# A top-2 mixture-of-experts kernel on one core: a rewritten prologue, three tiles with an fp32 down product, and a reordered last turn

## The chip, the core and the metric

The kernel runs on one core of one Trainium2 chip. The core's engines work side by side, each on its own queue of instructions in program order: TensorE (PE; its weight loads are PEld) multiplies into PSUM, VectorE (DVE), ScalarE (ACT) and GpSimd (POOL) do elementwise work, and DMAs are issued from the queues of SyncE (SP), ScalarE and GpSimd. Engines wait for each other by semaphores. The metric is the device time of one execution in microseconds (us); lower is better.

## What is computed

```python
# x (2,1024,256); weight (256,256); router_w (8,256); lang_w (4,256)
# w1 (8,256,1024), b1 (8,1024); w2 (8,1024,256), b2 (8,256)
ys = cond * 256**-0.5
d = rsqrt(einsum('bi,io->bo', ys*ys, weight*weight) + 1e-8)
y = einsum('bsi,io->bso', x * ys[:, None, :], weight) * d[:, None, :]
lang = softmax(y @ lang_w.T + lang_b);  lp = pad(lang, one zero)
idx = arange(8) % 4
logits = y @ router_w.T + router_b + 0.1 * (lp[..., idx] + lp[..., idx + 1])
top_p, top_i = top_k(softmax(logits), 2);  top_p = top_p / top_p.sum(-1)
h = gelu(einsum('bsd,edh->bseh', y, w1) + b1)        # exact gelu
expert_out = einsum('bseh,ehd->bsed', h, w2) + b2
out = x + sum over the two chosen experts of top_p * expert_out
```

## The kernel before

2048 tokens stand in 16 tiles of 128. Each goes to two of eight experts; the 4096 places are sorted by expert into 39 tiles of 128 (`NT`), some partly filled. Tile j of the first eight belongs to expert j, so that the code knows its expert; the other tiles look theirs up in the table `te`.

**Precision.** The large products are made of float16 pairs. Each weight matrix is a "half" n (n = 2e is w1 of expert e, n = 2e + 1 its w2), comes from HBM in fp32 (1 MB) into a staging place `PLACE[n]` and is split into a high part (`split_high`, ScalarE, L641) and a low part (`split_low`, VectorE, L779). Each needs a power-of-two scale, from a bound on the half: TensorE multiplies 16 column blocks with themselves (`gram`, L460), ScalarE sums (`gram_sums`), TensorE adds over partitions (`sum_squares`), VectorE makes the scale (`scale_weights`). The order of the low splits is `LOW_ORDER`. The hidden h of a tile is split likewise in two halves g of four chunks: GELU (L684), high part (`high_h`), low part (`low_h`, L945), both times a scale out of `cur`. A down product takes three float16 products of 256 columns a chunk (high by high, high by low, low by high); from tile 8 on two instructions cover them.

**Prologue.** SyncE loads cond, the adaLN weight, the router rows, x in four pieces of 512 KB, then halves 0 to 3; later ones wait for a place. Place 4 to 9 are laid over the buffers of x and of the prologue. TensorE transposes x in pairs of tiles (`transpose_x`, L411) and the router rows; VectorE forms the demodulation d, the combined weight Wyr (L747, L752), and TensorE computes the rows of y with their 12 logits (`rows_of_y`, L445), fp32. ScalarE squares x for the scale of y (`square_x`). y is split and written to `y_rows` in HBM. Then VectorE alone walks the routing: language softmax, two picks, counts per expert (through TensorE), the base of every expert's tiles, each token's slot (L869 to L878), two one-hot arrays (`tilehot`, `onehot`), which TensorE multiplies into the list `idx` of token numbers by slot (L510). The gates are computed between these steps on VectorE and written to `y_rows`. GpSimd gathers the rows of tile j by an indirect DMA (L350), five ahead.

**Main loop.** Turn j on TensorE: transpose tile j + 2 (L525, one PSUM bank, so it waits for the copy `copy_x` of the tile ahead), block up (j+1, 0) with down (j-1, 1), block up (j+1, 1) with down (j, 0); in turns 1 to 3 the Gram of one expert in the middle. Up (j, g) with j < 8 waits for split 2j of `LOW_ORDER`, down for split 2j + 1 and for the low part of h. VectorE's and ScalarE's turns are written out by hand at the end of their blocks. `rows_out` (L955, L960) scales the down result and adds b2; GpSimd multiplies by the gate (L368) and adds the rows to `out` by an indirect DMA (L373), one at a time. `expert_table(j)` copies the scales into `cur` and waits, from tile 3 on, until GpSimd's gate multiply of tile j - 3 is done (`o_ready`). The first scatter waits for the copy of x to `out` (`x_copied`).

## Time and profile before

| | |
|---|---|
| median of three runs | 326.2 us (326.15 to 326.49) |
| the profiled execution | 324.92 us, its span 323.1 us |
| PE busy | 280.9 us (87%) |
| ACT / DVE / POOL busy | 210.5 / 197.2 / 173.8 us |
| share of the chain that ended last | PE 65%, DMA 8%, DVE 7%, POOL 6%, issue 5%, ACT 5% |
| moved by DMA | 35.72 MB |

### The profile page before, as it was taken

What the parts mean: (1) busy time and instruction counts of PE and PEld (TensorE: products, weight loads), DVE (VectorE), ACT (ScalarE), POOL (GpSimd) and SP (SyncE); (2) the same over time, 40 slices, a digit from 0 to 9 for tenths busy, and PEclk for the clock granted to TensorE, in tenths of its full rate; (3) what the DMA queues carried; (4) which work ended last, traced back from release to release, by engine and by line L of the source; (5) the groups of instructions that cost most, each with busy time, mean ns of one, the idle gap of its engine ahead of it and who ended that gap; (6) DMA issues with size and microseconds to landing.
All of it is one profiled execution on the core that took longest, in us unless ns stands there. A gap on an engine that the chain in (4) does not pass through costs nothing.

```text
span 323.1 us, 9091 instructions
## 1 busy us (share of the span) xinstructions
PE 280.9 (87%) x3118; PEld 233.7 (72%) x3118; DVE 197.2 (61%) x461; ACT 210.5 (65%) x457; POOL 173.8 (54%) x140
## 2 busy tenths in 40 slices
PE   6889957859969966999999999999999999999900
PEld 4867856559859964888888888888888878888600
DVE  1227787479775895665756666665756666675610
ACT  2657489895669967767675757667675757667400
POOL 3040000640782896686677676768677675746460
PEclk9599985897989999999999999999999999999985
DMA  4987998189932112233323223242323223231220
GB/s 145 374 301 233 366 370 247 50 311 361 358 96 35 19 35 50 36 48 55 58 46 52 52 39 64 35 68 36 58 46 50 53 40 63 37 51 18 32 21 11
DMA packets 25480, 35.72 MB, mean 111 GB/s; under 512 B 4112, under 2 KB 21984, under 8 KB 25280
## 3 DMA queue, kind: packets, MB, share of 16 engines
q1 hardware_dynamic: 17584, 24.73, 22.2%
q0 software_dynamic: 7488, 10.39, 19.9%
q8 instruction: 29, 0.48, 0.6%
q10 hardware_dynamic: 368, 0.04, 0.1%
q14 instruction: 11, 0.09, 0.1%
HBM read 27.61 MB, written 9.64 MB: 115 GB/s over the span
## 4 chain that ended last, share of the span: by engine, by line
PE 65%; DMA 8%; DVE 7%; POOL 6%; issue 5%; ACT 5%; SPq 1%; ACTq 0%; DVEq 0%; POOLq 0%
PE ps L533 28%; PE ps L547 26%; POOL onehot L368 5%; PE ps L445 4%; DMA wsp<-in_L_ffn_w 4%; DVE wsp L779 3%; ACT wsp L641 3%; PE ps L525 2%; DMA out<-onehot,idx 2%; DMA wsp<-in_x 2%; PE ps L411 2%; ACT pay L684 1%; DVE pay L945 1%; POOL out L373 1%; PE ps L515 1%
## 5 line engine op out<-in xcount | busy, mean ns | idle before, releaser
L533 PE MATMUL ps<-onehot,wsp 128*128 128x128 f16 x1872 | 159.3, 221 | 7.0 <-DVE wsp L779 6.2
L533 PEld LDWEIGHTS ps<-onehot,wsp 128*128 (+1 forms) x1872 | 133.1, 97 | 37.9 <-DVE wsp L779 7.5
L684 ACT ACTIVATE pay<-ps,cur 128x128 f32<-128x128 f32 x312 | 117.4, 457 | 62.4 <-issue 43.6
L547 PE MATMUL ps<-wsp,pay 128*128 (+1 forms) x688 | 152.0, 313 | 0.1
L368 POOL TENSOR_SCALAR onehot<-onehot,cur 128x256 f32<-128x256 f32 x39 | 50.1, 1285 | 63.7 <-DVE onehot L960 34.4
L945 DVE SCALAR_TENSOR_TENSOR pay<-pay,cur 128x512 f16<-128x512 f32 x78 | 59.1, 757 | 40.6 <-ACT pay L673 38.5
L373 POOL DMA_INDIRECT out<-onehot,idx x39 | 71.2, 1827 | 14.1 <-POOL onehot L368 8.1
L350 POOL DMA_INDIRECT rows<-y_rows,idx x39 | 46.0, 1179 | 48.5 <-DVE idx L899 36.9
L547 PEld LDWEIGHTS ps<-wsp,pay 128*128 128x128 f16 x688 | 55.3, 97 | 3.1 <-issue 0.5
L673 ACT ACTIVATE pay<-pay,cur 128x512 f16<-128x512 f32 x47 | 34.0, 723 | 1.5
L939 DVE TENSOR_SCALAR pay<-pay,cur 128x512 f16<-128x512 f32 x31 | 17.5, 565 | 27.5 <-ACT pay L684 27.5
L955 DVE SCALAR_TENSOR_TENSOR onehot<-ps,cur,b2bc 128x256 f32<-128x256 f32 x39 | 18.8, 483 | 3.9 <-PE ps L547 2.4
L641 ACT ACTIVATE wsp<-stage,wscale 128x2048 f16<-128x2048 f32 x8 | 15.7, 1997 | 5.2 <-DVE wsp L779 4.0
L779 DVE SCALAR_TENSOR_TENSOR wsp<-wsp,wscale 128x2048 f16<-128x2048 f32 x8 | 18.8, 2347 | 0.0
L779 DVE SCALAR_TENSOR_TENSOR wsp<-stage,wscale,wsp 128x2048 f16<-128x2048 f32 x8 | 18.8, 2345 | 0.0
L525 PE MATMUL ps<-ident,rows 128*128 128x128 f32 x78 | 15.0, 274 | 3.1 <-DVE onehot L922 2.5
L460 PE MATMUL ps<-wsp 128*128 128x128 bf16 x128 | 11.5, 263 | 7.0 <-DMA wsp<-in_L_ffn_w 6.2
L445 PE MATMUL ps<-wsp,pay 128*128 128x268 f32 x64 | 16.3, 397 | 1.4 <-DVE wsp L803 0.7
L641 ACT ACTIVATE wsp<-wsp,wscale 128x2048 f16<-128x2048 f32 x8 | 15.7, 2000 | 1.1 <-DVE wscale L772 1.0
L460 PEld LDWEIGHTS ps<-wsp 128*128 128x128 bf16 x128 | 10.4, 120 | 7.6 <-DMA wsp<-in_L_ffn_w 4.5
L960 DVE SCALAR_TENSOR_TENSOR onehot<-ps,cur,onehot 128x256 f32<-128x256 f32 x31 | 15.0, 484 | 1.1
L525 PEld LDWEIGHTS ps<-ident,rows 128*128 128x128 f32 x78 | 9.7, 144 | 7.1 <-issue 3.5
(164 smaller groups left out, 181.9 us busy)
## 6 DMA issues: line engine op xcount, KB each, us to landing
stage<-in_L_ffn_w SPq DMA_DIRECT2D x8, 1024.0 KB, 11.5
wsp<-in_L_ffn_w SPq DMA_DIRECT2D x8, 1024.0 KB, 10.4
wsp<-in_x SPq DMA_DIRECT2D x4, 512.0 KB, 8.1
y_rows<-pay SPq DMA_DIRECT2D x4, 512.0 KB, 10.3
b2bc<-in_L_ffn_b SPq DMA_DIRECT2D x1, 1024.0 KB, 10.2
rows<-y_rows,idx POOLq DMA_INDIRECT x39, 2.9
out<-onehot,idx POOLq DMA_INDIRECT x39
wsp<-in_L_cond_weight SPq DMA_DIRECT2D x1, 256.0 KB, 2.9
```

The source lines that it names most:

```text
L350: g.indirect_dma_start(out=rows[:, j % ROWS, :], out_offset=None, in_=y_rows, in_offset=bass.IndirectOffsetOnAxis(ap=idx[:, j:j + 1], axis ...
L368: g.tensor_scalar(outb[:, j % RING, :], outb[:, j % RING, :], cur[:, j % RING, C_P:NCUR], None, ALU.mult).then_inc(o_ready, 1)
L373: g.indirect_dma_start(out=out, out_offset=bass.IndirectOffsetOnAxis(ap=idx[:, j:j + 1], axis=0), in_=outb[:, j % RING, :], in_offset=None ...
L445: last = mm(ps[:, t % BANKS_Y, 0:WIDTH_Y], xT[:, t, k * P:(k + 1) * P], Wyr[:, t // TB, k, :], start=(k == 0), stop=(k == KD - 1))
L525: last = tr(ps[:, XB, k * P:(k + 1) * P], rows[:, j % ROWS, k * P:(k + 1) * P], ident[:, :])
L533: last = mm(ps[:, HB + (2 * j + g) % RING, c * P:(c + 1) * P], wsp[:, bass.ds(e, 1), o:o + P].rearrange("p a f -> p (a f)"), xsp[:, j % RI ...
L547: last = mm(ps[:, OB + j % 2, 0:width], hsp[:, (2 * j + g) % NH, part, c, :], wsp[:, bass.ds(e, 1), o + w:o + w + width].rearrange("p a f ...
L641: a.activation(parts_of(n)[0], staged(n), ACT.Copy, scale=wscale[:, n:n + 1]).then_inc(w_high, 1)
L673: a.activation(hsp[:, (2 * j + g) % NH, 0, :, :].rearrange("p c n -> p (c n)"), h32[:, g, :], ACT.Copy, scale=cur[:, j % RING, C_H:C_H + 1 ...
L684: last = a.activation(h32[:, g, c * P:(c + 1) * P], ps[:, HB + (2 * j + g) % RING, c * P:(c + 1) * P], ACT.Gelu, bias=cur[:, j % RING, cc: ...
L779: v.scalar_tensor_tensor(out=lo, in0=staged(n), scalar=wscale[:, n:n + 1], in1=hi, op0=ALU.mult, op1=ALU.subtract).then_inc(w_split, 1)
L945: v.scalar_tensor_tensor(out=lo, in0=h32[:, g, :], scalar=cur[:, j % RING, C_H:C_H + 1], in1=hi, op0=ALU.mult, op1=ALU.subtract).then_inc( ...
```

## The change

- **x** comes in five pieces (2, 2, 4, 4, 4 tiles). A tile now holds the tokens p * 8 + t of a batch instead of t * 128 + p, so that a partition's tiles are adjacent in HBM. cond and the router rows are issued on ScalarE's queue, b1 and the biases on SyncE's behind x.
- **Start**: the router rows are transposed ahead of x, R is copied behind dcol. The scale of y comes from the largest |x| (`max_of_x`, five VectorE reductions) instead of ScalarE's squares. Tile pair 4 of x is transposed among the rows of y. GpSimd's large iota waits for nothing.
- **Loads**: halves 0, 2, 4, 6, 1, 7 at once; 3 after the first piece of y is written; 8, 9, 5 after the last; b2's broadcast, which stood behind half 5, after three gathers; then 10 to 13, the copy of x to `out`, 14 and 15. Half 14 waits for split_low(10), half 15 for split_low(11).
- **Grams** in groups of two or three halves (`GROUPS`); two groups ahead of the routing, two after the mapping, three in the loop (turns 1, 2, 4). From the third group on VectorE takes the largest entry (`gram_max`) instead of ScalarE's sum. Warm products 6 instead of 12.
- **Routing**: bases by five steps over an 8 x 8 mask instead of logarithmic sums; TensorE also adds the home tile; onehot last, in four pieces; gates on GpSimd and ScalarE, written to `y_rows` from ScalarE's queue.
- **Tiles 0 to 2** (`DIRECT`): the down product is one fp32 product of 256 columns per chunk, of the unsplit GELU result and the staged w2. No high_h, no low_h, no wait for splits 1, 3, 5; those follow later, in `SPLIT_ORDER`.
- high_h(j, 1) is on VectorE for all tiles from 3 on (before from 8 on).
- **Last turn**: rows_out(37) is VectorE's first step of turn 38, and the gates of tiles 37 and 38 are multiplied on ScalarE (`weigh`).

The core of the diff:

```diff
-WARM = 12
-PLACE = (0, 1, 2, 3, 4, 5, 6, 7, 8, 9, 0, 2, 4, 5, 1, 3)
-LOW_ORDER = (0, 2, 1, 4, 3, 6, 5, 8, 7, 10, 9, 12, 11, 14, 13, 15)
+WARM = 6
+DIRECT = 3
+PLACE = (0, 7, 1, 4, 2, 5, 3, 6, 8, 9, 0, 1, 2, 3, 0, 1)
+SPLIT_ORDER = (0, 2, 4, 6, 7, 8, 1, 9, 10, 11, 12, 13, 3, 5, 14, 15)
+SPLITS = {0: (6, 7), 1: (8, 1), 2: (9, 10), 3: (11, 12), 4: (13, 3), 5: (5, 14), 6: (15,)}
+HIGHS = {0: (8, 1), 1: (9, 10), 2: (11, 12), 3: (13, 3), 4: (5,), 5: (14, 15)}
+GROUPS = ((0, 2, 4), (6, 7), (8, 9), (1, 3, 5), (10, 11), (12, 13), (14, 15))
+GRAMS = {1: 4, 2: 5, 4: 6}
...
 # SyncE, behind the loads of 8, 9 and 5
             for j in range(RING):
                 sp.wait_ge(gathered[j], 16)
+            sp.dma_start(b2bc[:, :, :].rearrange("p e d -> p (e d)"), ...)
+            for n in (10, 11, 12, 13):
+                load_weights(n)
             for b in range(NB):
                 sp.dma_start(out[b * SEQ:(b + 1) * SEQ, :], x[b]).then_inc(x_copied, 16)
-            for n in (10, 11, 14, 12, 15, 13):
+            for n in (14, 15):
                 load_weights(n)
...
 # TensorE, down_step and its waits
+                if j < DIRECT:
+                    return mm(ps[:, OB + j % 2, 0:D], hraw[:, (2 * j + g) % NH, c, :], staged(2 * j + 1)[:, cc, :],
+                              start=(cc == 0), stop=(cc == KF - 1))
...
+                    if j < DIRECT:
+                        pe.wait_ge(w_in[PLACE[2 * j + 1]], 16)
+                        pe.wait_ge(gelu_done, 2 * j + g + 1)
...
 # ScalarE, split_high
+                if n in (12, 13):
+                    wait_split(act, 8)
+                    wait_split(act, 9)
+                if n in (14, 15):
+                    wait_split(act, 3)
+                    wait_split(act, 5)
+                    act.wait_ge(l2_done, 3)
...
 # GpSimd, the gates
+            pool.wait_ge(best, 1)
+            g.tensor_tensor(pex, lg[:, :, 0:E], over(s1[:, 3, :], E), ALU.subtract).then_inc(p_in, 1)
+            pool.wait_ge(second, 1)
+            g.tensor_tensor(pe1[:, 0, :], s1[:, 4, :], s1[:, 3, :], ALU.subtract).then_inc(p_in, 1)
+            pool.wait_ge(p_exp, 2)
+            g.tensor_scalar(pe1[:, 2, :], pe1[:, 1, :], 1.0, None, ALU.add).then_inc(p_sum, 1)
...
 # VectorE, the counts to the bases
+            step(v.tensor_scalar(tl[:, 0, :], ps[:, 3, 0:E], -(P / 2 + 0.5), 1.0 / P, ALU.add, ALU.mult))
+            step(v.tensor_scalar(tl[:, 1, :], tl[:, 0, :], MAGIC, MAGIC, ALU.add, ALU.max))
+            step(v.scalar_tensor_tensor(out=tmask[:, :, :], in0=tl[:, 1:2, :].broadcast_to([P, E, E]), scalar=-MAGIC,
+                                        in1=before[:, :, :], op0=ALU.add, op1=ALU.mult))
+            step(v.tensor_reduce(base[:, 0, :], tmask[:, :, :], AX.X, ALU.add))
+            step(v.tensor_tensor(base[:, 1, :], base[:, 0, :], over_base[:, :], ALU.add))
...
 # VectorE, the turns
             for j in range(NT):
-                if j >= EARLY:
+                if j == NT - 1:
+                    rows_out(j - 1)
+                if j >= DIRECT:
                     high_h(j)
-                low_h(j, 1)
+                    low_h(j, 1)
```

Where things stand in a row, at three places.

VectorE at the start, before: the copy of R (it waits for the router rows' transposition, which is behind x on TensorE) is ahead of the root chain.

```order
L729 TENSOR_SCALAR dv<-ps 128x4
L731 COPY R<-ps 128x24
L733 RECIPROCAL dv<-dv 128x4
L734 TENSOR_TENSOR dv<-dv 128x4
L735 TENSOR_TENSOR dv<-dv 128x4
L736 TENSOR_SCALAR dv<-dv 128x4
L738 TENSOR_TENSOR dcol<-dv 128x4
L742 TENSOR_TENSOR Rd<-R,dcol 128x2x12 x2
L747 SCALAR_TENSOR_TENSOR wsp<-wsp,ys,ps 128x256 x4
```

And after:

```order
L784 TENSOR_SCALAR dv<-ps 128x4
L786 RECIPROCAL dv<-dv 128x4
L787 TENSOR_TENSOR dv<-dv 128x4
L788 TENSOR_TENSOR dv<-dv 128x4
L789 TENSOR_SCALAR dv<-dv 128x4
L791 TENSOR_TENSOR dcol<-dv 128x4
L794 COPY R<-ps 128x24
L797 TENSOR_TENSOR Rd<-R,dcol 128x2x12 x2
L802 TENSOR_REDUCE xmax<-wsp 128x1 x2
L810 SCALAR_TENSOR_TENSOR wsp<-wsp,ys,ps 128x256 x4
```

R moved behind dcol, and two reductions of x came ahead of Wyr.

VectorE at the end of the routing, before (wsp is `tilehot` in L884 and L887), where TensorE's mapping products wait for L887:

```order
L876 TENSOR_REDUCE slot<-wsp 128x32
L877 TENSOR_SCALAR slot<-slot 128x32
L878 TENSOR_SCALAR slot<-slot 128x32
L884 TENSOR_TENSOR wsp<-wsp,slot 128x1248
L885 TENSOR_TENSOR onehot<-wsp,slot 128x4096
L887 TENSOR_TENSOR wsp<-wsp,tok 128x1248
```

And after:

```order
L939 TENSOR_REDUCE slot<-wsp 128x32
L940 TENSOR_SCALAR slot<-slot 128x32
L941 TENSOR_SCALAR slot<-slot 128x32
L947 TENSOR_TENSOR wsp<-wsp,slot 128x1248
L949 TENSOR_TENSOR wsp<-wsp,tok 128x1248
L953 TENSOR_TENSOR onehot<-wsp,slot 128x128x8 x4
```

onehot moved to the end and became four pieces.

ScalarE from the GELUs (5, 0) of turn 4 on, before (L684 GELUs, L673 high_h, L669 copy_x, L631 gram_sums, L641 split_high, here of halves 14 and 15):

```order
L684 ACTIVATE pay<-ps,cur 128x128 x4
L673 ACTIVATE pay<-pay,cur 128x512
L641 ACTIVATE wsp<-stage,wscale 128x2048
L684 ACTIVATE pay<-ps,cur 128x128 x4
L673 ACTIVATE pay<-pay,cur 128x512
L669 ACTIVATE onehot<-ps 128x256
L684 ACTIVATE pay<-ps,cur 128x128 x4
L673 ACTIVATE pay<-pay,cur 128x512
L641 ACTIVATE wsp<-stage,wscale 128x8x256
```

And after, from the same GELUs on (L736 GELUs, L724 high_h, L720 copy_x, L695 split_high of 14 and 15):

```order
L736 ACTIVATE pay<-ps,cur 128x128 x4
L724 ACTIVATE pay<-pay,cur 128x512
L736 ACTIVATE pay<-ps,cur 128x128 x4
L720 ACTIVATE onehot<-ps 128x256
L695 ACTIVATE wsp<-stage,wscale 128x2048
L736 ACTIVATE pay<-ps,cur 128x128 x4
L724 ACTIVATE pay<-pay,cur 128x512
L695 ACTIVATE wsp<-stage,wscale 128x8x256
```

The high split of half 14 moved from turn 4 to turn 5, ahead of the GELUs (6, 0), and high_h of (5, 1) left this queue.

## Rows read from the trace of the kernel before

**Rows 1.** TensorE's waits: what waited for whom, total us, times, longest.

```profile
PE ps L533 <- DVE wsp L779: 6.2, 4, 3.3
```

**Rows 2.** Timeline of the start: start us, us, engine, line, operation, [idle before].

```profile
2.42 2.25 SPq L285 DMA_DIRECT2D wsp<-in_x  x4
...
6.45 0.21 ACT L601 ACTIVATE dv<-dv 128x4 f32<-128x4 f32 x1 [0.60 <-DVE dv L729]
...
9.16 1.94 PE L411 MATMUL ps<-ident,wsp 128*128 128x128 f32 x8 [2.95 <-DMA wsp<-in_x]
...
15.06 1.65 DVE L747 SCALAR_TENSOR_TENSOR wsp<-wsp,ys,ps 128x256 f32<-128x256 f32 x4 [2.11 <-PE ps L428]
...
17.15 2.04 PE L445 MATMUL ps<-wsp,pay 128*128 128x268 f32 x8 [0.68 <-DVE wsp L752]
...
22.72 0.55 ACT L646 ACTIVATE pay<-ps,yscale 128x256 f16<-128x256 f32 x1 [3.25 <-DVE yscale L762]
...
37.00 0.22 DVE L813 TENSOR_REDUCE s<-wsp 128x16 f32<-128x64 f32 x1
```

**Rows 3.** Timeline from the routing chain to the first gathered rows.

```profile
40.88 0.16 DVE L770 TENSOR_SCALAR wround<-ps 128x2 f32<-128x2 int32 x1
...
44.79 0.16 DVE L845 TENSOR_SCALAR tli<-ps 128x8 int32<-128x8 f32 x1
...
50.40 2.29 DVE L885 TENSOR_TENSOR onehot<-wsp,slot 128x4096 f16<-128x4096 int16 x1
...
53.46 2.85 PE L510 MATMUL ps<-wsp,onehot 128*128 128x39 f16 x32 [0.23 <-DVE wsp L887]
...
56.72 0.20 DVE L899 SCALAR_TENSOR_TENSOR idx<-ps,wsp 128x39 uint32<-128x39 f32 x1
...
57.86 2.37 POOL L350 DMA_INDIRECT rows<-y_rows,idx  x1 [36.91 <-DVE idx L899]
...
60.99 2.75 PE L515 MATMUL ps<-onehot,ones 128*128 128x512 f16 x12
...
63.58 0.38 PE L525 MATMUL ps<-ident,rows 128*128 128x128 f32 x2
```

**Rows 4.** Busy time by stretch (PE, PEld, DVE, ACT, POOL), TensorE's clock, DMA share, GB/s.

```profile
58.00:60.00 2.00, 1.72 (x17) 1.45 (x14) 1.17 (x1) 2.00 (x2) 2.00 (x1) 0.59 0.00 0
```

**Rows 5.** Groups by line, 63.4 to 135 us: count, busy us, mean ns, idle before.

```profile
L684 ACT ACTIVATE pay<-ps,cur 128x128 f32<-128x128 f32 x68 | 25.5, 455 | 7.9 <-PE ps L533 4.4 <-DVE cur L932 2.1 <-issue 1.4
L779 DVE SCALAR_TENSOR_TENSOR wsp<-wsp,wscale 128x2048 f16<-128x2048 f32 x8 | 18.8, 2347 | 0.0
...
L945 DVE SCALAR_TENSOR_TENSOR pay<-pay,cur 128x512 f16<-128x512 f32 x16 | 11.9, 746 | 11.0 <-ACT pay L673 10.0 <-issue 1.1
...
L641 ACT ACTIVATE wsp<-wsp,wscale 128x2048 f16<-128x2048 f32 x4 | 8.0, 1999 | 1.1 <-DVE wscale L772 1.0
```

**Rows 6.** Timeline of turns 2 to 7, TensorE.

```profile
92.39 1.09 PE L460 MATMUL ps<-wsp 128*128 128x128 bf16 x16 [3.04 <-DMA wsp<-in_L_ffn_w]
...
97.63 0.28 PE L465 MATMUL ps<-wsum,ones 128*128 128x2 f32 x2
...
119.95 0.52 PE L533 MATMUL ps<-onehot,wsp 128*128 128x128 f16 x6 [0.78 <-DVE wsp L779]
...
120.63 0.51 PE L533 MATMUL ps<-onehot,wsp 128*128 128x128 f16 x6
...
128.66 0.41 PE L525 MATMUL ps<-ident,rows 128*128 128x128 f32 x2 [2.50 <-DVE onehot L922]
```

**Rows 7.** DMA: issues with median us to landing; spread of the weight loads' line.

```profile
out<-in_x SPq DMA_DIRECT2D x2, 8.1
...
DMA to landing us min/median/max: 4.9/11.3/14.0
```

**Rows 8.** Last turn: scatter 36 in the timeline, scatter 37 in the chain of waits.

```profile
302.97 1.83 POOL L373 DMA_INDIRECT out<-onehot,idx  x1 [0.28 <-POOL onehot L368]
...
308.01 3.69 DMA out<-onehot,idx
```

More of the change, by code:

```diff
@@ L120, in adaln_moe @@
         first = sb("first", [P, E], I32)
-        home = sb("home", [P, E], I32)
+        eids = sb("eids", [P, E], I32)
+        homes = sb("homes", [P, E], F16)
+        over_base = sb("over_base", [P, E], I32)
+        before = sb("before", [P, E, E])
         tok1 = sb("tok1", [P, K * T], I32)
@@ L574, in _ @@
             transpose_rows(0)
+            sum_squares(2)
             transpose_rows(1)
@@ L871, in _ @@
-            step(v.tensor_tensor(r2[:, :, :], rank, eq[:, :, :], ALU.add))
-            step(v.tensor_tensor(eq[:, :, :], r2[:, :, :], each(home[:, :]), ALU.add))
+            step(v.scalar_tensor_tensor(out=eq[:, :, :], in0=ps[:, RB, 0:T * E].rearrange("p (t e) -> p t e", e=E),
+                                        scalar=float(P), in1=each(base[:, 1, :]), op0=ALU.is_ge, op1=ALU.mult))
+            step(v.tensor_tensor(eq[:, :, :], ps[:, RB, T * E:2 * T * E].rearrange("p (t e) -> p t e", e=E), eq[:, :, :],
+                                 ALU.add))
```

498 lines of the change are left out of this document (269 added, 229 removed).

## The prediction

> **What bounds the kernel now.** First the table of TensorE's waits [rows 1]: in 323.1 us it waits for others only near the start and in the first eight turns; from 130 us on no wait is listed. A faster start therefore shifts everything behind it, and a change of the first turns is worth what it does to the moment at which the waits end. The timeline then gives four marks. The combined weight Wyr is ready and the rows of y begin at 17.15; VectorE's routing chain begins at 37.00; the indices are written at 56.72 to 56.92; the first gathered rows are transposed at 63.58 [rows 2, 3]. I forecast each mark. Below, u is the time since the first transposes of gathered rows. Before, turn 7 begins with its transposes at 128.66, u = 65.1 [rows 6], and turn 8 begins at u = 71.5 (transposes and a wait to 129.73, then two blocks of 2.7).
>
> **To the rows of y.** Before, TensorE sits 2.95 us and starts on x at 9.16; behind that on its queue stands the transposition of the router rows, and behind that VectorE's copy of R and the whole root chain, so the 1.65 us that build Wyr run from 15.06 only [rows 2]. After, the router rows go ahead of x and R behind dcol. The root that dcol needs is taken at 6.45 [rows 2], so it comes near 7.5. x in pieces of 256 KB is issued 1.2 us sooner than the first 512 KB before (2.42 [rows 2], and three small loads less ahead). What remains is x: TensorE must do pieces 0 and 1 before the dcol products (1.9 us at the low clock, 0.9 at the high one), and piece 2 before the router products. New on VectorE are five reductions of x, two ahead of Wyr, of 512 elements each; the products of Wyr take 0.41 for 256 [rows 2], so between 0.41 and 0.82, and I take 0.6. With x there at 6 to 7.5 us: transposes to 9, dcol products to 10, Wyr 1.65 and its router part, 12 us; 11 if nothing is late, 14.5 if the clock falls as it did before. I take 12.5, since the router rows are now third on ScalarE's queue and could land late. **Gain 4.4 (2.5 to 5.9).**
>
> **The rows of y.** Before, 17.15 to 37.00: 5.6 us to the first scaled tile (22.72) and 14.3 of tiles bound by TensorE [rows 2]. After, three reductions of x (1024 elements, by the same row 0.8 to 1.6, taken as 1.1 each) stand ahead of the scale, which TensorE's own queue mostly hides (it reaches that place 3.2 us after the start, they take 3.5), plus one small multiply; and one more transposition pair (0.45) falls among the tiles. Cost 0.8. The routing chain begins at 33.3: 12.5 + 20.8. **Gain 3.7 (1.5 to 5.5).**
>
> **The routing chain, 19.9 us before.** Step by step on VectorE [rows 3]: the first scale_weights inside the first pick goes (0.35). The second scaling, the third and the gap subtraction leave the place between the choice and the counts: the counts are taken at 44.79, 0.9 after the choice, and what stands there now (a reciprocal 0.25, one scaling 0.45) is as long as the way over TensorE, gain about 0.1. From the counts to the table of bases 2.7 us of 14 small steps become five steps of 0.16 to 0.25, 1.15: gain 1.55. One of the full-width adds goes (0.33), as TensorE adds the home tile itself; its 33 products instead of 16 take 1.5 us and end just ahead of the bases, at no cost. Then tilehot, its multiply and onehot were 3.75 us before TensorE's 32 mapping products (2.85) could start [rows 3]. Now onehot (2.29) comes last in four pieces, and eight products follow each piece: after the last piece 0.7 remains instead of 2.85, with about 0.4 for three more instructions and the wait. Gain 1.75. Sum 4.1; I take 3.6, as products (0.71 per eight at the low clock) are longer than pieces (0.6). ScalarE's part must not be late: GpSimd subtracts, ScalarE takes two exponentials, GpSimd adds, all beside the second pick, and the reciprocal has about 1 us to spare. The indices at 16.3 after the chain's start: 49.6. **Gain 7.3 in all.**
>
> A row and a rule: the first gather lasted 2.37 us instead of 0.96 beside a split_low that began before it [rows 3]. The Trainium skill, "SBUF — State Buffer", section Who interferes with whom, says that a VectorE instruction with two SBUF inputs shuts out GpSimd instructions that read SBUF, but infers that descriptor writing isn't shut out. The row speaks for the wider reading. By the rule alone the gather would save 1.4 us, hidden by the next term, and the sum stays.
>
> **From the indices to the first transposes, 6.7 before.** Two things run: the gather (0.9 until it starts, then held by split_low(0), which in the new order begins about 1.4 after the indices: data some 6.3 to 6.6 after them) and TensorE's own queue. That now holds five Gram halves (8, 9, 1, 3, 5) and six warm products. The clock was low when the mapping products began at 53.46 and rose about 6 us later [rows 3, 4]; again TensorE has little to do from the choice on, so I take it as low, and as rising about 6.2 us after the first mapping products. That makes 1.8 halves at 1.9 us and 3.2 at 0.96, and six warm products at 0.23 [rows 3]: 7.9 after the mapping, 7.3 after the indices. TensorE is last, not the gather. Cost 0.7. First transposes at 56.9. **Gain 6.6 (3 to 9).**
>
> **The first turns.** Prices [rows 5]: split_low 2.35 (VectorE), split_high 1.94 back to back (ScalarE), low_h 0.75, four GELUs 1.5; six up and three down products 0.67 [rows 6], so a block 2.7. The down product of tiles 0 to 2 in fp32: one pass of 256 columns for each of eight chunks. The row of fp32 products with 268 columns gives 0.46 each [rows 2], so 0.44 and 3.5 a tile against 2.7: TensorE gets 0.8 more three times. Hidden, since TensorE waits there anyway. It takes away the waits for splits 1, 3 and 5, and six low_h. But all 16 splits are still due by turn 7, and 11 of ScalarE's are now left at u = 0, where before it were 7: the five high splits after routing end 5 us before the rows come, and ScalarE then stands still.
>
> I followed the three queues with these prices, in u. ScalarE from 3.0: GELUs, copies and splits 8, 1, 9, 10, 11 end with high_h(3) at 25.8. VectorE: splits 2, 4, 6, 7, 8, 1 until 17.8, tables to 19.3, then expert_table(3), which needs tile 0's scatter path and so the copy of x to the output. VectorE's low_h(3,0) waits for 25.8 anyway; split_low(10) and the scales of 12 and 13 end 29.5; only then may ScalarE split 12 and go on to the GELUs of (3,1), which end 33. VectorE stood still 3 us. From 33 it is full: two parts of h, splits 11, 12, 13, 3, 5, tables: 54.2. ScalarE may not split 14 before split 5 is low (53.7), and GELUs (6,0) come behind that: h(6,0) at 57.8, low_h 58.6, **split_low(14) ends at u = 61**, 3.6 us of standing still included. Turn 6 of TensorE waits for exactly this from 52.6 on; before, the like wait ended at 119.95, u = 56.4. After it, the old order lost another 3.9 us (split 13, then VectorE's copy_x(8) with a 2.5 us wait) [rows 1, 6]; the new one has nothing left but one split and runs two turns of 5.6. Turn 8 then begins at 72.2, plus the low clock after an 8 us wait. Before, after 3.04 us of waiting, half a Gram and a block took 5.2 (92.39 to 97.63) instead of 3.7 [rows 6], 1.5 more; I take 1.8 (1.5 to 3.1). So turn 8 at u = 74.0 against 71.5: **loss 2.5**.
>
> **The steady turns** are unchanged. **The last turn**: scatters form a chain, 302.97 then 308.01, each 3.7 to landing and 0.75 to the next start [rows 8]. With rows_out(37) ahead of the last split and ScalarE's multiply in place of GpSimd's, scatter 37 can start at 302.97 + 4.45 = 307.4. The last down product comes 0.65 later through the same move, still ahead of its scatter. **Gain 0.6.** That the tiles take tokens eight apart changes addresses of gathers and scatters, not their number: nothing, or up to 0.3 us per scatter, hidden but for two.
>
> **Sum**: -6.6 + 2.5 - 0.6 = -4.7 (rounded up) against the profiled execution, 324.9 to 320.2. The median of the runs is 326.2, 1.3 above that execution; the same difference gives 321.5.
>
> **Rivals.** A, the loop fits together better than by hand. For: of the 61 us to split_low(14) VectorE works 51; the 10 us of standing still are couplings that shift with small delays. If half goes, split_low(14) ends at 56 and turn 8 begins near 68: 315.5. If all goes, TensorE's own 52.6 decides, turn 8 begins at 63.8: 311.3. B, slower than before: the copy of x to the output. Before, it was issued right after three gathers and took 8.1 us [rows 7]. Now it stands behind b2's broadcast and four weight loads, the last of which waits for split_low(6) (u = 9.4), so 7 MB are under way from u = 4. At the rate of the weight loads (about 400 GB/s) it lands at 22, which is where VectorE can still bear it (22.7). Every us beyond that delays expert_table(3) and all behind it one for one: from 27 the gain is gone, and at 250 GB/s it lands at 32: 331. C, the start doesn't get shorter: x is not there sooner, or TensorE's clock falls in the start; then nothing of the 3.7 is left at the routing chain, the rest as above: 325.2. One DMA more: the load of half 15 waits for split_low(11) (36.8) and needs 4.9 at least [rows 7]; its Gram comes at 42, TensorE waits 4 us in turn 4, and this is inside the calculation, because VectorE is later still.
>
> **Chances.** Forecast (319 to 325) 0.52; A (311 to 318) 0.25; C 0.10; B 0.13. A measurement of this kernel can tell 0.2% (0.65 us) from no change; by the same cases faster 0.79, same 0.07, slower 0.14. The range 313 to 327.5 leaves out the far end of A and half of B, and a slow loop beside a slow start.
>
> **What would show it.** The y rows should begin at 12.5 and the routing chain near 33; the indices 16.3 after that; TensorE's clock low in the mapping; the first transposes at 57, right behind the warm products, with no wait for the gather. In the turns, VectorE should be idle before high_h(3) and before low_h(6,0), and TensorE's longest wait should be for split_low(14) in turn 6. If VectorE is instead idle at expert_table(3) for long, it is B. If turn 8 begins under 70 us after the first transposes, my reading of the couplings is wrong and A holds. If the y rows begin after 15, the first term is wrong.

## The result, and the profile after

| | median, us | runs |
|---|---|---|
| before | 326.12 (323.71 to 328.05) | 20 |
| after | 323.89 (321.89 to 326.9) | 20 |

The ratio is 0.994, with a 95% interval of 0.9919 to 0.996: the change makes the kernel 1.3 to 2.6 us faster. (The ratio leaves out three of the changed kernel's 20 runs, which lay over 1.5% above its fastest.) In a later group of runs it was 0.9958 (0.9925 to 0.999). The forecast of 321.5 us had the sign right and the size more than twice too large: 4.7 us less were forecast, some 2 are there, and 1.4 by the later group.

The profiled execution of the changed kernel took 323.72 us, with a span of 321.9. TensorE's waits, with total us, times and longest us, say where it now stands still (L553 is the mapping at the end of the routing and L527 a step among the rows of y, the other three are in the turns):

```profile
PE ps L576 <- DVE wsp L852: 7.4, 1, 7.4
PE ps L553 <- DVE onehot L953: 4.4, 1, 4.4
PE ps L496 <- DMA stage<-in_L_ffn_w: 3.4, 1, 3.4
...
PE ps L568 <- DMA rows<-y_rows,idx: 1.8, 1, 1.8
PE ps L527 <- DVE bmx L859: 1.2, 1, 1.2
```

[Rows 1] showed four waits for splits (L779 there, L852 here) with 3.3 us as the longest. Now there is one of 7.4 us. The timeline shows the marks up to the first gathered rows, to be read beside [rows 2, 3]:

```profile
12.88 2.04 PE L482 MATMUL ps<-wsp,pay 128*128 128x268 f32 x8 [0.41 <-DVE wsp L815]
...
27.26 0.27 PE L527 MATMUL ps<-ident,bmx 128*8 128x128 f32 x1 [1.24 <-DVE bmx L859]
...
34.85 0.22 DVE L891 TENSOR_REDUCE s<-wsp 128x16 f32<-128x64 f32 x1
...
51.31 0.20 DVE L962 SCALAR_TENSOR_TENSOR idx<-ps,wsp 128x39 uint32<-128x39 f32 x1
...
57.09 1.46 PE L558 MATMUL ps<-onehot,ones 128*128 128x512 f16 x6
58.38 0.38 PE L568 MATMUL ps<-ident,rows 128*128 128x128 f32 x2
```

And the same timeline at turns 1 to 6, in order of time, ScalarE's, VectorE's and TensorE's rows together:

```profile
82.99 0.17 DVE L1005 COPY cur<-tab 128x11 f32<-128x11 f32 x1 [5.34 <-POOL onehot L406]
...
89.45 2.00 ACT L695 ACTIVATE wsp<-stage,wscale 128x2048 f16<-128x2048 f32 x1 [3.94 <-DVE wscale L845]
...
101.83 1.47 PE L496 MATMUL ps<-stage 128*128 128x128 bf16 x16 [3.41 <-DMA stage<-in_L_ffn_w]
...
113.38 2.00 ACT L695 ACTIVATE wsp<-stage,wscale 128x2048 f16<-128x2048 f32 x1 [4.67 <-DVE wsp L852]
...
117.56 0.75 DVE L1019 SCALAR_TENSOR_TENSOR pay<-pay,cur 128x512 f16<-128x512 f32 x1 [3.87 <-ACT pay L724]
118.23 2.34 DVE L852 SCALAR_TENSOR_TENSOR wsp<-stage,wscale,wsp 128x2048 f16<-128x2048 f32 x1
...
120.63 0.82 PE L576 MATMUL ps<-onehot,wsp 128*128 128x128 f16 x6 [7.41 <-DVE wsp L852]
...
128.66 0.38 PE L568 MATMUL ps<-ident,rows 128*128 128x128 f32 x2
...
134.27 0.38 PE L568 MATMUL ps<-ident,rows 128*128 128x128 f32 x2
```

Turn 7 begins at 128.66 us in both of these profiles [rows 6]: all that the prologue won, 5.2 us at the first transposes, has been paid back by then. Turn 8 begins at 134.27 instead of 135.2, because the old order lost time once more in turn 7 (the wait at 128.66 in [rows 6]). The last scatter starts at 311.26.

### The profile page after: what moved, and what is told of

Its sections match the earlier page's. It is cut to its first block, busy times and chain, and to the rows that moved or that the text cites. A ratio compares the mean times of both kernels' runs of the same rounds, so it can differ in the third digit from the quotient of the medians.

```text
span 321.9 us, 9020 instructions
## 1 busy us (share of the span) xinstructions
PE 281.6 (87%) x3103; PEld 234.6 (73%) x3103; DVE 201.4 (63%) x462; ACT 195.9 (61%) x419; POOL 164.9 (51%) x145
## 4 chain that ended last, share of the span: by engine, by line
PE 49%; POOL 16%; issue 10%; DVE 9%; DMA 9%; ACT 2%; SPq 1%; POOLq 0%; DVEq 0%; ACTq 0%
PE ps L576 20%; PE ps L593 18%; POOL out L413 8%; POOL onehot L406 5%; PE ps L482 4%; DMA out<-onehot,idx 4%; DMA out<-in_x 4%; POOL rows L387 3%; DVE wsp L852 3%; DMA wsp<-in_x 2%; PE ps L496 2%; PE ps L568 2%; SPq L338 1%; PE ps L455 1%; PE ps L553 1%
## 5 line engine op out<-in xcount | busy, mean ns | idle before, releaser
L736 ACT ACTIVATE pay<-ps,cur 128x128 f32<-128x128 f32 x312 | 117.3, 460 | 65.8 <-issue 49.6
L593 PE MATMUL ps<-wsp,pay 128*128 (+1 forms) x616 | 140.6, 318 | 1.2 <-DVE pay L1019 1.2
L1019 DVE SCALAR_TENSOR_TENSOR pay<-pay,cur 128x512 f16<-128x512 f32 x72 | 54.7, 760 | 36.1 <-ACT pay L724 34.8
L406 POOL TENSOR_SCALAR onehot<-onehot,cur 128x256 f32<-128x256 f32 x37 | 36.8, 994 | 76.4 <-DVE onehot L1037 39.9
L593 PEld LDWEIGHTS ps<-wsp,pay 128*128 128x128 f16 x616 | 49.4, 98 | 3.9 <-issue 1.6
L695 ACT ACTIVATE wsp<-stage,wscale 128x2048 f16<-128x2048 f32 x10 | 19.8, 2002 | 13.6 <-DVE wscale L845 7.1
L724 ACT ACTIVATE pay<-pay,cur 128x512 f16<-128x512 f32 x36 | 26.0, 722 | 1.2
L852 DVE SCALAR_TENSOR_TENSOR wsp<-stage,wscale,wsp 128x2048 f16<-128x2048 f32 x10 | 23.4, 2344 | 0.0
L585 PE MATMUL ps<-wsp,pay 128*128 128x256 f32 x48 | 15.5, 405 | 0.0
L1005 DVE COPY cur<-tab 128x11 f32 (+2 forms) x39 | 6.8, 175 | 12.0 <-POOL onehot L406 7.3
L852 DVE SCALAR_TENSOR_TENSOR wsp<-wsp,wscale 128x2048 f16<-128x2048 f32 x6 | 14.1, 2344 | 0.0
## 6 DMA issues: line engine op xcount, KB each, us to landing
wsp<-in_L_ffn_w SPq DMA_DIRECT2D x6, 1024.0 KB, 12.4
```

The costliest lines, as they stand in the source:

```text
L406: g.tensor_scalar(outb[:, j % RING, :], outb[:, j % RING, :], cur[:, j % RING, C_P:NCUR], None, ALU.mult).then_inc(o_ready, 1)
L593: last = mm(ps[:, OB + j % 2, 0:width], hsp[:, (2 * j + g) % NH, part, c, :], wsp[:, bass.ds(e, 1), o + w:o + w + width].rearrange("p a f ...
L695: a.activation(parts_of(n)[0], staged(n), ACT.Copy, scale=wscale[:, n:n + 1]).then_inc(w_high, 1)
L724: a.activation(hsp[:, 2 * j % NH, 0, :, :].rearrange("p c n -> p (c n)"), h32[:, 0, :], ACT.Copy, scale=cur[:, j % RING, C_H:C_H + 1]).the ...
L736: last = a.activation(to, ps[:, HB + (2 * j + g) % RING, c * P:(c + 1) * P], ACT.Gelu, bias=cur[:, j % RING, cc:cc + 1], scale=cur[:, j % ...
L852: v.scalar_tensor_tensor(out=lo, in0=staged(n), scalar=wscale[:, n:n + 1], in1=hi, op0=ALU.mult, op1=ALU.subtract).then_inc(w_split, 1)
```

## A second profile of both kernels

One profiled execution of each kernel turned out to be a thin base, so both were run and profiled once more, unchanged, in one group.

> The changed kernel once more, unchanged, as the one against which the others of this group are read, and to see whether its profiled execution was a typical one. The profiles of four kernels that share its first 18 us differ there: the first rows of y began at 12.88 us in its own, at 14.3, 14.4 and 14.3 in three of the others, and in those TensorE's transposes of x still took 1.06 us a pair at 11 to 13.5 us where its own took 0.60. Theory S (TensorE's pace at the start rises at one moment or another, launch by launch, and the profile of the changed kernel caught an early one): a second profile shows either 12.9 and a first scaled tile at 19.3, or 14.3 and 21.6, and the prologue's gain of some 4.3 us on y is 1.4 to 2.4 us less in many executions. Rival (the four edited kernels moved something at the start): 12.9 and 19.3 again. Time either way 323.9, ratio 0.994.

> The kernel before, unchanged, for a second profile beside the second one of the changed kernel, taken on the same chip: where each kernel's y rows begin, its routing chain starts, its indices are ready and its eighth turn begins. If the moment at which TensorE's pace rises at the start scatters here too, the first profile's 17.15 us and 37.00 us move by 1 to 2 us; if the old start has a wait long enough that the pace is always low until the same row, they repeat within 0.3 us. Ratio 1.000.

Measured: 324.58 us for the changed kernel (12 runs, ratio 0.9958, 0.9925 to 0.999), 325.08 for the kernel before (12 runs, ratio to the other runs of itself 0.9985, 0.9953 to 1.0017). The marks, read from the two timelines of each kernel, in us:

| mark | before, 1st and 2nd | after, 1st and 2nd | forecast |
|---|---|---|---|
| rows of y begin | 17.15, 15.30 | 12.88, 14.36 | 12.5 |
| routing chain begins | 37.00, 35.16 | 34.85, 37.20 | 33.3 |
| indices written | 56.72, 54.84 | 51.31, 53.62 | 49.6 |
| first transposes of gathered rows | 63.58, 63.74 | 58.38, 60.98 | 56.9 |
| turn 8 begins | 135.20, 135.08 | 134.27, 135.14 | 130.9 |
| last scatter starts | 312.46, 312.41 | 311.26, 312.28 | - |

Theory S holds for what varies: the start moves by 1.5 to 2.4 us from launch to launch, in both kernels. In the kernel before, the granted clock shows it: it is 0.50 from 9 to 15 us in the first profile, and 1.00 from 12 us on in the second, where x also came 0.7 us sooner (transposes from 8.45 instead of 9.16). In the changed kernel the products show it. TensorE's transposes of the third and fourth pair of x in the first profile of the changed kernel, and then in the second:

```profile
10.59 0.60 PE L455 MATMUL ps<-ident,wsp 128*128 128x128 f32 x4
```

```profile
11.05 1.06 PE L455 MATMUL ps<-ident,wsp 128*128 128x128 f32 x4
13.47 1.09 PE L455 MATMUL ps<-ident,wsp 128*128 128x128 f32 x4
```

Yet the busy table of the second profile (PE, PEld, DVE, ACT, POOL, then TensorE's granted clock, DMA share, GB/s) gives a granted clock of 1.00 there:

```profile
9.00:12.00 3.00, 3.00 (x16) 2.82 (x14) 2.40 (x8) 0.60 (x1) 0.00 (x0) 1.00 0.98 346
12.00:15.00 3.00, 3.00 (x15) 2.87 (x15) 2.27 (x7) 0.99 (x2) 0.00 (x0) 1.00 0.89 362
```

The column can't be taken at its word here: in the profile of the kernel that multiplies first (an experiment below) the same transposes take the same time, and it reads 0.50:

```profile
13.43 1.09 PE L455 MATMUL ps<-ident,wsp 128*128 128x128 f32 x4
```

```profile
12.00:15.00 3.00, 3.00 (x15) 2.87 (x14) 2.27 (x7) 1.03 (x2) 0.00 (x0) 0.50 0.81 328
```

So at the start I read the clock's level (1.2 or 2.4 GHz) from the pace of the products, 1.06 us a pair or 0.60, and not from that column. Of the ten profiles of kernels that share the new start, four rose before 11 us, five only after 14.5, one between. In two of the five (the kernel that multiplies first and the last one below) it is not a late rise but a fall: the four transposes at 4.1 us still took 0.60, and the granted clock then fell at about 7.5 us and stayed at 0.50 until past 17. The Trainium skill, "TensorE: Matmul & The Clock Gate", section Part 1: The HAM clock gate, says that the number of slow products at a kernel's start differs from run to run of one kernel and costs less than 1% of a typical span. Both agree with these profiles; but 2 us of 324 are 0.6%, as much as this whole change.

## Experiments on the turns

Marks are given from the kernel's own first transposes on, which takes the scatter of the start out: u is the time since them, as in the prediction. The eighth turn begins at u = 71.6 and 71.3 before, 75.9 and 74.2 after. All kernels below are the changed kernel with one edit, compared with the kernel before in 6 to 12 runs each.

**GpSimd's multiply ahead of the wait for the copy of x** (rival B of the prediction).

```diff
-                if j == 0:
-                    pool.wait_ge(x_copied, 16 * NB)
                 if j < NT - 2:
                     ... multiply ...
+                if j == 0:
+                    pool.wait_ge(x_copied, 16 * NB)
                 ... scatter ...
```

> The changed kernel, but GpSimd multiplies tile 0's output before it waits for the copy of x, and waits for that copy only ahead of the scatter. VectorE's expert_table(3) needs the multiply alone; in the changed kernel it came at 82.99 us after 5.34 us of idle time. Theory F (what starts late in turn 1 is still late in turn 6): VectorE is idle for 5.3 us at 77.6, and behind it only for 1.6, 1.7, 0.4 us up to 113.7. With the table at 77.6, split_low(9) ends at 80.1, the maxima of halves 12 and 13 still wait for their products at 81.7, scale_weights(5) comes at about 86 instead of 88.97, split_high(12) at 86.4 instead of 89.45, the load of half 15 is issued 3 us earlier (93.5), the 3.4-us wait for it at 101.83 is nearly gone, and the eighth turn starts 2.5 to 3 us earlier: 321.1 us beside 323.9 of the changed kernel. Theory L (only the last links count: split_low(5), split_high(14), the GELUs, split_low(14)): VectorE catches up by itself and the gain is 0 to 0.7 us. If the copy itself is what delays the loads behind it (half 14's, half 15's), nothing moves either, since it is still there.

Measured: 322.86 us, ratio 0.9927 (0.9894 to 0.9961), not to be told from the changed kernel. VectorE's 5.34 us of idle time at expert_table(3) is gone, but the wait of turn 6 ends at u = 61.4, against 62.3 and 61.7 in the two profiles of the changed kernel: 0.3 to 0.9 us arrives. The timeline of this kernel shows why:

```profile
86.71 0.75 DVE L1019 SCALAR_TENSOR_TENSOR pay<-pay,cur 128x512 f16<-128x512 f32 x1 [2.06 <-ACT pay L724]
...
90.20 2.00 ACT L695 ACTIVATE wsp<-stage,wscale 128x2048 f16<-128x2048 f32 x1 [3.52 <-DVE wscale L845]
```

VectorE now waits for ScalarE's high part of tile 3 instead, as the prediction's walk had it ("low_h(3,0) waits for 25.8 anyway"). Theory F falls, and with it rival B as the cause: the copy of x landed at u = 23.6 in the first profile, 0.9 past the point that the prediction named, and its price is no more than that, 0.3 to 0.9 us.

**The scales of halves 12 and 13 ahead of a split.**

```diff
+                if j == 2:
+                    scale_weights(GRAMS[j])
                 for n in SPLITS.get(j, ())[1:2]:
                     split_low(n)
-                if j in GRAMS:
+                if j in GRAMS and j != 2:
                     scale_weights(GRAMS[j])
```

> The changed kernel, but in turn 2 VectorE computes the scales of halves 12 and 13 (scale_weights(5)) before split_low(10) and not behind it. In the changed kernel their sums of squares were on TensorE at 85.86 us, the scales came at 88.97 behind a split of 2.35 us, and ScalarE idled 3.94 us for them before split_high(12) at 89.45. Theory: the scales come at 87.0, split_high(12) starts at 87.4, the GELUs (3, 1) and split_low(11) come 2 us earlier, half 15's load is issued at 94.4 instead of 96.5 and TensorE's 3.4-us wait for it at 101.83 shrinks to 1.4 us. But TensorE's wait for gather 6 at 94.37 stays where it is, and turn 6's wait of 7.4 us stands behind split_low(12), (13), (3) and (5), with which VectorE is busy from 97.9 to 113.7: it is late by what these are late. If they move with it, the eighth turn starts 2 us earlier: 321.9. Rival: VectorE's splits of turns 3 to 5 wait for TensorE's turns, not for ScalarE; the 2 us are absorbed in them and the gain is 0.3 to 0.8 us: 323.3. I take the rival at even odds, since freeing 5.3 us on VectorE in turn 1 moved the eighth turn by only 0.9.

Measured: 323.53 us, ratio 0.9918 (0.988 to 0.9956); the second profile's group had the changed kernel at 0.9958, so the runs alone don't settle it. The profile does: the wait of turn 6 ends at u = 60.3 instead of 62.3 and 61.7, 1.4 to 2.0 us earlier; turn 8 begins at u = 73.3, 2.6 less than in the changed kernel's profile with the same early start (some 0.6 of it is a shorter low clock), and the last scatter at 308.78 instead of 311.26. The wait for half 15's load is 1.04 instead of 3.41, and split_low(14) starts 1.7 us earlier, in a launch that began 0.2 later:

```profile
87.34 2.00 ACT L695 ACTIVATE wsp<-stage,wscale 128x2048 f16<-128x2048 f32 x1 [1.68 <-DVE wscale L845]
...
101.55 1.09 PE L496 MATMUL ps<-stage 128*128 128x128 bf16 x16 [1.04 <-DMA stage<-in_L_ffn_w]
...
116.51 2.35 DVE L852 SCALAR_TENSOR_TENSOR wsp<-stage,wscale,wsp 128x2048 f16<-128x2048 f32 x1
...
118.91 0.82 PE L576 MATMUL ps<-onehot,wsp 128*128 128x128 f16 x6 [7.57 <-DVE wsp L852]
```

I had leaned to the rival, wrongly. Two small instructions (0.4 us) that stand behind one split of 2.35 us delay the whole of turns 2 to 6; TensorE's wait isn't shorter, it only comes and ends earlier.

**Tile 6's GELUs ahead of split_high(14).**

```diff
-HIGHS = {..., 4: (5,), 5: (14, 15)}
+HIGHS = {..., 4: (5,), 5: (None, 14, 15)}
...
+                    if n is not None:
+                        split_high(n)
```

> The changed kernel, but in turn 5 ScalarE evaluates the GELUs of tile 6 before it copies the high part of half 14 (both halves 14 and 15 then stand behind the GELUs). In the changed kernel ScalarE stood idle for 4.67 us until split_low(5) was done at 113.3, copied for 2.0, evaluated for 1.5 and converted for 0.7, and VectorE had to idle 3.87 us for that before low_h(6, 0) at 117.56 and split_low(14) at 118.23. Theory L (the last links set turn 6): the GELUs run in ScalarE's idle time at 110 to 113, low_h(6, 0) follows rows_out at 113.7, split_high(14) still starts at 113.4, and split_low(14) starts at 115.4 instead of 118.23: TensorE's wait at 120.63 falls from 7.4 to 4.6 us and the end by 2.8 us, to 321.1. Rival C (the clock): TensorE has still idled for over 3 us and still runs its next 5 us at the low clock, and split_high(15), now directly behind split_high(14), delays the GELUs (6, 1) by 2 us into a new wait: the gain is 1.0 to 1.5 us, 322.6. Rival F (the chain is late from turn 1 on): the same 2.8 us as theory L here, since both edits act on one chain in series; it differs at the kernel that multiplies first.

Measured: 320.95 us, ratio 0.9851 (0.9811 to 0.989), the only single edit whose interval lies clear of the changed kernel's. TensorE's wait is 2.7 us shorter:

```profile
115.90 3.89 ACT L695 ACTIVATE wsp<-stage,wscale 128x2048 f16<-128x2048 f32 x2 [1.17 <-DVE wsp L853]
...
120.35 0.82 PE L576 MATMUL ps<-onehot,wsp 128*128 128x128 f16 x6 [4.72 <-DVE wsp L853]
```

Turn 6's products resume at u = 59.2, against 62.3 and 61.7 in the two profiles of the changed kernel, as theory L had it; no new wait for the GELUs (6, 1) stands in their place. So the last link of the chain was ScalarE's order: GELUs that could run in 4.67 us of idle time stood behind a copy that could not.

**TensorE kept busy in the wait of turn 6.**

```diff
+                if j == 6:
+                    pe.wait_ge(w_scaled, 7)
+                    keep_warm(30, 7, 512)
                 blocks((j + 1, 0) if j + 1 < NT else None, (j - 1, 1) if j else None)
```

> The changed kernel, but TensorE runs 30 products of 512 columns on constants into a bank that nobody reads, behind the transposes of tile 8 in turn 6, that is in the 7.4 us in which it waits for split_low(14); they change no output. At the high pace of 0.21 us each they last 6.4 us and end before the wait does. Theory K (the wait costs more than its length: after it TensorE ran eight pairs of steps at 1.28 us a pair instead of 0.67, 2.6 us in all, at a granted clock of 0.50): the granted clock in 120 to 126 us is 1.0, the steps take 0.67 us a pair, the eighth turn starts 2.6 us earlier, 321.3 us. Rival V (VectorE and ScalarE bind after the wait: split_low(15) at 123.46, the GELUs (6, 1) and low_h(6, 1)): TensorE runs at the high clock but waits again for them, and of the 2.6 us some 1 to 1.5 arrive: 322.6. Rival Z (no effect): the clock falls all the same.

Measured: 321.56 us, ratio 0.9898 (0.9846 to 0.995). That interval overlaps the changed kernel's, so the profile has to decide. Turn 8 begins at u = 74.2, 1.7 less than in the first profile of the changed kernel but the same as in the second; split_low(14) itself ended 0.7 and 1.2 us later here than in those, so the time behind it is what tells. The busy table of the changed kernel (its granted clock is the 0.50), then the products in this kernel's timeline, then its busy table (1.00):

```profile
120.00:126.00 6.00, 5.37 (x39) 4.58 (x40) 5.67 (x17) 1.43 (x5) 0.00 (x0) 0.50 0.01 3
```

```profile
114.81 6.69 PE L424 MATMUL ps<-ones 128*128 128x512 f16 x30
```

```profile
120.00:126.00 6.00, 6.00 (x70) 5.00 (x69) 5.83 (x16) 3.27 (x9) 0.00 (x0) 1.00 0.01 4
```

From the end of the 30 products (121.50) to turn 8 it takes 10.8 us; the changed kernel took 13.6 and 12.4 from the end of its wait. Theory K holds in the traces: after the wait of 7 us the low clock costs 1.6 to 2.8 us, by launch. Some 0.5 us of it was lost again, as 30 products were a few too many: split_low(14) had ended at 121.0.

**ScalarE's copies of x later among the rows of y.**

```diff
-                if t in (0, 2, 4):
-                    copy_xt(5 + t // 2)
+                if t in (0, 5, 8):
+                    copy_xt({0: 5, 5: 6, 8: 7}[t])
```

> The changed kernel, but ScalarE copies the seventh and eighth pair of transposed x tiles after the sixth and ninth tile of y instead of after the third and fifth. In the changed kernel ScalarE idled 1.19 us at 21.61 and 1.22 us at 24.25 for transposes that TensorE now makes two tiles later than before, VectorE idled 1.59 and 1.62 us behind it, and TensorE then waited 1.24 us at 27.26 for the bias maxima. Theory Y: these are one stall; TensorE's wait of 1.24 us goes, the y phase takes 20.8 us instead of 22.0, the routing chain starts at 33.6 instead of 34.85, and the end comes 1.0 to 1.2 us earlier: 322.8 us. Rival (the y phase is bound by TensorE's own 20 us of products and transposes): the idle times shift between ScalarE and VectorE, and the chain starts within 0.3 us of 34.85; no change of time. Rival (the loads behind the loop's start take the gain): the chain starts at 33.6 but the expert tables still wait for the copy of x, and of the 1.2 us under 0.4 arrive at the end.

Measured: 323.58 us, ratio 0.9935 (0.9901 to 0.9969). From VectorE's part of the first scaled tile (19.28 in the changed kernel's first profile) to the routing chain it takes 14.10 us instead of 15.57 (15.56 or 15.57 in all seven profiles with the old copies). But this launch was one with a late start (rows of y at 14.31), so the mark is no earlier than the 34.85 of the changed kernel's first profile, and 1.5 us earlier than the 37.20 of its second, which started as late:

```profile
35.69 0.22 DVE L891 TENSOR_REDUCE s<-wsp 128x16 f32<-128x64 f32 x1
```

Theory Y holds for the trace. That 1.5 us reach the end was not shown by this kernel alone, with an interval of 2 us on its runs.

**Tokens numbered as before.**

```diff
-x_tiles = x.rearrange("b (p t) d -> p b t d", p=P)
+x_tiles = x.rearrange("b (t p) d -> p b t d", p=P)
... (y_tiles likewise) ...
-g.iota(tok1[:, :], pattern=[[0, K], [SEQ, NB], [1, TB]], base=1, channel_multiplier=TB)
+g.iota(tok1[:, :], pattern=[[0, K], [P, T]], base=1, channel_multiplier=1)
```

> The changed kernel with the old meaning of a tile of tokens: partition p and tile t hold token 128 t + p, as before, instead of 8 p + t within a batch; x, the scaled rows and the token numbers all go by it. Theory G (the new numbering lengthens the indirect transfers: consecutive slots of an expert tile lie eight tokens apart): the median landing of a gather falls from 3.4 to 2.9 us, the scatters' from 4.0 to 3.7, the tail behind the last product gets 0.2 to 0.3 us shorter, and TensorE's wait of 1.8 us for gather 6 by 0.5; against it, x now comes in pieces of 1 KB and y goes out in pieces of 1 KB, which may cost 0.2 to 1 us at the start (x tiles land later than 6.94 and 8.33). Sum: between -0.8 and +0.7 us on 323.9, I take +0.1. Rival (landing times depend on what runs beside them, not on the numbering): the gathers' median stays at 3.4, and only the price at the start shows, +0.5.

Measured: 323.22 us, ratio 0.9959 (0.9925 to 0.9994). The median landings stay long (columns: count, median us from issue to landing), so theory G falls, and no price shows at the start either (the rows of y begin at 13.04):

```profile
rows<-y_rows,idx POOLq DMA_INDIRECT x39, 3.8
out<-onehot,idx POOLq DMA_INDIRECT x39, 4.0
```

The second pair of profiles says the same from the other side: with the new numbering the changed kernel's gathers have a median of 3.4 and then 2.9, and the kernel before, 2.9 both times, has 4.0 for its scatters in its second profile.

**All four orders, and the products on top.** The edits of the multiply, the scales, the GELUs and the copies together; then the same with 18 warm products in turn 6.

> The changed kernel with the four changes of order together: GpSimd multiplies tile 0's output before it waits for the copy of x, VectorE computes the scales of halves 12 and 13 before split_low(10), ScalarE evaluates tile 6's GELUs before split_high(14), and it copies the seventh and eighth pair of x tiles later. Alone they moved the eighth turn against the first transposes by 0.9, 2.4 and 3.05 us, and the routing chain by 1.4 us against the first scaled tile. Theory A (one chain in series: scales of half 12, load of half 15, splits 12, 13, 3, 5, then the high and low part of half 14, so that what is saved at different links adds up): from the first transposes to the eighth turn 75.9 - 2.4 - 3.0 - 0.5 (the first and second save the same idle time on ScalarE in part) = 70.0 us, and with 1.4 us less ahead of it the end comes 6.5 to 7 us earlier than the changed kernel's: about 317.3 us. Rival T (TensorE's own work and the low clock take over as the waits shrink: some 5 us of idle time still stand before the eighth turn, and gather 6 and the load of half 15 do not move with VectorE): 3.5 to 4.5 us, 319.8 us.

> The four orders as in the other kernel of this group, and 18 products of 512 columns on constants on TensorE in the wait of turn 6 (4.0 us at 0.22 each; they change no output). Alone, 30 of them behind the changed kernel's own order kept the granted clock at 1.0 and brought 2.4 us from split_low(14) to the eighth turn. Theory A: the wait left by the orders is 4.5 to 5 us, the 18 products fill it, and the steps behind it take 0.67 us a pair from the first: 2.0 to 2.6 us less than the four orders alone, about 315 us. Rival T: the wait has shrunk under 3 us, the clock would have stayed up or VectorE's split_low(15) binds next, and the products themselves stand on the path: within 0.7 us of the four orders, or slower by up to 1 us.

Measured: 316.86 us, ratio 0.9754 (0.9709 to 0.9799), and 314.30 us, ratio 0.966 (0.9621 to 0.9699). Turn 8 begins at u = 69.9 (theory A: 70.0) and at 67.2. The waits of turn 6, of the first and of the second kernel:

```profile
113.51 0.82 PE L576 MATMUL ps<-onehot,wsp 128*128 128x128 f16 x6 [5.71 <-DVE wsp L853]
```

```profile
111.19 4.08 PE L424 MATMUL ps<-ones 128*128 128x512 f16 x18
115.73 0.52 PE L576 MATMUL ps<-onehot,wsp 128*128 128x128 f16 x6 [0.46 <-DVE wsp L856]
```

So the savings add up along one chain, as theory A has it, and the kernel with both is 3.4% faster than before, over five times what the change brought. What is left in the turns is a wait of 3.6 us for half 15's load. The rise of TensorE's pace at the start remains a matter of the launch: the profile of the 316.86 us kernel caught an early one (315.37 us), that of the 314.30 us kernel one of the two with the fall, and so a late one (316.29 us).

## Why the prediction was off, step by step

The marks and their order were right, and so was the wait that decides the turns. Two terms of the sum failed. The rows of y were booked as costing 0.8 us and cost 2.1 and 3.0 more than before, as ScalarE's copies among them had been put at nothing. The first turns were booked as a loss of 2.5 us and lost 4.3 and 2.8. Most of the rest is TensorE's clock in the start, which differs from launch to launch in both kernels: the rows of y begin 0.4 and 1.9 us later than forecast, and 1.9 us earlier than I took them to in the old kernel's second profile.

- **To the rows of y**: forecast 12.5 us, measured 12.88 and 14.36. The order of work is as described. I had 14.5 for a clock that falls as before. In the second profile the rows do begin near there, but by another way: the pace is low from the start and rises only after 14.5 us. A fall stands in two of the ten profiles, where they begin at 14.3 and 14.4. What I lacked was a forecast of how often either happens. I also took 17.15 of the old kernel as fixed, where its second profile has 15.30. The gain here is 4.3 between the first profiles and 0.9 between the second ones.
- **The rows of y**: 20.8 forecast, 22.0 and 22.8 measured. This term was mis-sized: I charged the extra transposes of x with TensorE's 0.45 us and kept ScalarE's copies at no cost. They stood in ScalarE's order one and two tiles too early; it idled 1.19 and 1.22 us for them, VectorE 1.6 us twice behind it, and TensorE 1.24. The kernel with later copies shows 1.5 us. The further 0.9 us of the second profile lies ahead of the first scaled tile (7.28 us from the first row of y instead of 6.40). ScalarE's copies in the first profile:

```profile
21.61 0.60 ACT L660 ACTIVATE pay<-ps 128x512 f32<-128x512 f32 x1 [1.19 <-PE ps L455]
24.25 0.60 ACT L660 ACTIVATE pay<-ps 128x512 f32<-128x512 f32 x1 [1.22 <-PE ps L455]
```

- **The routing chain**: 16.3 forecast, 16.46 and 16.42 measured, against 19.7 before. Right in sum. One part was not: TensorE's products for the bases, booked at no cost, held VectorE for 0.69 us at a granted clock of 0.50. In three of the ten profiles that wait is absent and the chain takes 15.8 us.

```profile
43.83 0.29 DVE L932 SCALAR_TENSOR_TENSOR wsp<-ps,base 128x128 f32<-128x128 f32 x1 [0.69 <-PE ps L546]
```

- **Indices to first transposes**: 7.3 forecast, 7.07 and 7.36 measured; TensorE is last, right behind its warm products. Right. It hid one thing: the kernel before reached this mark at 63.58 and 63.74, though its indices came 1.9 us apart, so the gain up to this mark is 5.2 and 2.8 against the forecast 6.6. The old kernel's clock did that: it rose before 60 us in the first profile and only at 63 in the second, so its twelve warm products took 4.52 us instead of 2.75. Its busy table, first and second profile:

```profile
60.00:62.00 2.00, 1.25 (x7) 0.73 (x8) 0.76 (x5) 1.05 (x6) 1.40 (x3) 1.00 0.25 68
```

```profile
60.00:62.00 2.00, 2.00 (x6) 0.71 (x5) 0.79 (x5) 1.96 (x1) 1.70 (x2) 0.50 0.46 116
```

- **The first turns**: a loss of 2.5 forecast, 4.3 and 2.8 measured. The mechanism, its place and its wait were right, and its size was not: split_low(14) ends at u = 62.2 and 61.7 instead of 61, and 0.3 to 0.9 us of that goes with the wait for the copy of x. Turn 8 follows at 75.9 and 74.2 instead of 74.0; the low clock took 2.8 and 1.6 us instead of 1.8. But the walk took each queue's order as given. It found both stops (3 us behind the scales of 12 and 13, 3.6 behind split 14), and I booked them as couplings; one swap at each brought 1.4 to 2.0 and 2.5 to 3.1 us. Rival A, "the loop fits together better than by hand", had the right arithmetic for a kernel that wasn't built: with those two stops and the wait for the copy of x reordered away, turn 8 begins at 69.9, near A's 68. For the kernel as it was built, A is ruled out.
- **The tail**: 0.6 forecast, 0.25 measured (from turn 8 to the last scatter 177.26 and 177.33 before, 176.99 and 177.14 after). The first of the last two steps took 4.70 us and 4.79 instead of the 4.45 that I took from the kernel before: the scatters land 3.8 to 4.0 us after their issue rather than 3.7, and they stand in a chain:

```profile
302.01 1.82 POOL L413 DMA_INDIRECT out<-onehot,idx  x1 [0.28 <-POOL onehot L406]
306.71 1.56 POOL L413 DMA_INDIRECT out<-onehot,idx  x1 [2.88 <-DMA out<-onehot,idx]
311.26 1.55 POOL L413 DMA_INDIRECT out<-onehot,idx  x1 [2.99 <-DMA out<-onehot,idx]
```

Sum by marks: at the last scatter -1.2 and -0.13 us in the two pairs of profiles, and about -2 and -1.4 in the two groups of runs. The later landings are not shown to come from the change: the kernel before has 3.79 us for scatter 37 in its second profile, and the medians of one kernel move from profile to profile (gathers 3.4 and then 2.9 in the changed one). Why they do is open. Open too is what makes the pace rise early or late at the start, or fall there in some launches.

## What to carry to other kernels

When hand-walking coupled queues shows an engine standing still, ask at each stop which instruction it waits for and what stood ahead of that one on its own queue; four changes of order brought 1.9% here, the whole rewritten start and its companions 0.4 to 0.6%. A gain ahead of a loop counts only as far as the loop's own first chain lets it through, so measure it behind that chain, by marks relative to the loop's start. And profile both kernels twice before pricing a start to the microsecond.
